# Score products of a transformer kernel: two 64-row strips per half of the heads, or four 32-row strips for both halves together

## The reference

```python
q = jnp.einsum('bsd,hdk->bhsk', query, Wq) + bq[None, :, None, :]
k = jnp.einsum('bsd,hdk->bhsk', key, Wk) + bk[None, :, None, :]
v = jnp.einsum('bsd,hdk->bhsk', value, Wv) + bv[None, :, None, :]
scores = jnp.einsum('bhqk,bhsk->bhqs', q, k) / jnp.sqrt(jnp.asarray(D_K, q.dtype))
attn = jax.nn.softmax(scores, axis=-1)
heads = jnp.einsum('bhqs,bhsk->bhqk', attn, v)
...
x = x + _L3_xattn_ref(_layernorm(x, axis=-1), ctx_1024, ctx_1024, L3_xattn_Wq, ...)
```

## Time and profile before

| | |
|---|---|
| median of 3 runs | 892.31 us (890.75 to 893.44) |
| profiled execution, its own time | 890.07 us |
| its span, first to last instruction | 888.3 us |
| PE busy | 683.0 us, 77% |
| DVE, ACT, POOL busy | 441.4, 284.9, 291.2 us |
| score products L493 | 72.5 us of records, 256 of them |
| granted TensorE clock, mean of the span | 0.837 |

### The profile page before, as it was taken

The page is one execution under the profiler, slowest core; times in us unless marked ns, Lnnn a source line. Parts: engine busy times, 40 slices in busy tenths (PEclk is TensorE's granted clock), DMA queues, the critical chain, the costliest instruction groups (busy, mean ns, idle before and its releaser), DMA issues.

```text
span 888.3 us, 15004 instructions
## 1 busy us (share of the span) xinstructions
PE 683.0 (77%) x5836; PEld 424.0 (48%) x5836; DVE 441.4 (50%) x1182; ACT 284.9 (32%) x477; POOL 291.2 (33%) x324
## 2 busy tenths in 40 slices
PE   6799733999997879997687997497657937774974
PEld 3355521774555455655344465254424533443442
DVE  5566478554444695556464465433143333233332
ACT  3133310123333424443243343133314422341432
POOL 7122211113211242322645221353254316432542
PEclk9899855899998769998598999588759866895898
DMA  6900060031000000000105300120111012101212
GB/s 141 321 2 2 25 189 8 18 130 60 1 2 1 1 0 1 1 1 22 40 23 144 85 1 2 39 39 28 39 31 36 22 33 39 31 30 30 37 33 66
DMA packets 43756, 38.98 MB, mean 44 GB/s; under 512 B 11648, under 2 KB 34720, under 8 KB 43560
## 3 DMA queue, kind: packets, MB, share of 16 engines
q1 hardware_dynamic: 37240, 26.88, 10.4%
q0 software_dynamic: 5120, 10.50, 5.3%
q10 hardware_dynamic: 1328, 0.66, 0.3%
HBM read 30.75 MB, written 7.27 MB: 43 GB/s over the span
## 4 chain that ended last, share of the span: by engine, by line
PE 66%; DVE 15%; issue 8%; DMA 4%; ACT 3%; POOL 2%; another core or an unknown queue 2%; DVEq 0%; ACTq 0%; POOLq 0%
PE psum L1586 9%; PE psum L1609 8%; PE psum L535 8%; PE psum L493 7%; PE psum L1596 5%; PE psum L557 4%; PE psum L482 3%; PE psum L782 2%; PE psum L569 2%; PE psum L1178 2%; PE psum L690 2%; PE psum L578 2%; DVE scr L906 1%; DVE scr L872 1%
## 5 line engine op out<-in xcount | busy, mean ns | idle before, releaser
L288 POOL TENSOR_TENSOR scr<-KT,hmask 128x512 f32<-128x512 f32 x64 | 67.7, 1064 | 160.3 <-PE psum L535 64.0
L405 DVE TENSOR_REDUCE Mp<-psum 128x8 f32<-128x1024 f32 x64 | 78.5, 1226 | 65.9 <-PE psum L493 28.3
L1460 DVE COPY scr<-psum 128x512 f32<-128x512 f32 x64 | 44.2, 691 | 133.7 <-PE psum L1596 102.9
L312 ACT ACTIVATE scr<-psum 128x1024 f32<-128x1024 f32 x64 | 65.5, 1023 | 121.0 <-PE psum L535 44.7
L535 PE MATMUL psum<-Qa,scr 64*128 64x128 f32 x1024 | 74.1, 285 | 0.0
L493 PE MATMUL psum<-scr 64*128 64x512 f32 x256 | 72.5, 643 | 0.0
L535 PEld LDWEIGHTS psum<-Qa,scr 64*128 64x128 f32 x1024 | 63.5, 189 | 15.6 <-issue 10.4
L1596 PEld LDWEIGHTS psum<-ident,scr 128*128 128x128 f32 x304 | 36.3, 156 | 71.3 <-issue 65.9
L1342 POOL DMA_INDIRECT yb_d<-scr,tok x44 | 42.9, 974 | 55.0 <-ACT scr L1290 49.9
L1586 PE MATMUL psum<-big,xsT 128*64 128x512 f32 x144 | 48.5, 758 | 11.8 <-issue 4.2
L1596 PE MATMUL psum<-ident,scr 128*128 128x128 f32 x304 | 56.8, 316 | 1.0 <-ACT scr L1282 0.8
(11 more groups left out here) (341 smaller groups left out, 1220.7 us busy)
## 6 DMA issues: line engine op xcount, KB each, us to landing
big<-in_L_ffn_W SPq DMA_DIRECT2D x2, 2048.0 KB, 9.0
big<-in_L_ffn_W SPq DMA_DIRECT2D x8, 512.0 KB, 9.8
big<-in_L_ffn_W SPq DMA_DIRECT2D x1, 4096.0 KB, 13.7
b1r<-in_L_ffn_b SPq DMA_DIRECT2D x1, 2048.0 KB, 10.9
scr<-yb_d SPq DMA_DIRECT2D x6, 256.0 KB, 3.1
xn_d<-xn SPq DMA_DIRECT2D x2, 512.0 KB, 3.2
scr<-ya_d SPq DMA_DIRECT2D x4, 256.0 KB, 3.0
yb_d<-scr,tok POOLq DMA_INDIRECT x44
```

What stands on the lines that cost most here:

```text
L288: pool.tensor_tensor(Km[:, i % 2, c, :, :], KT[:, c, i, :].unsqueeze(1).to_broadcast([P, HV, P]), hmask4[:, :].unsqueeze(2).to_broadcast([ ...
L312: act.activation(PT[i % 2][:, c, :], pair(weights_unit(i, c)), ACT.Exp, scale=SCALE).then_inc(S(f"exp{c}"), 1)
L405: dve.tensor_reduce(Mp[:, HC * c:HC * c + HC, DH:DH + 1], pair(scores_unit(i, c)).rearrange("p (j k) -> p j k", j=HC), AX.X, ALU.max, nega ...
L1460: ins = dve.tensor_copy(hTg[:, g % 2, :], bank[[3, 6][g % 2]])
```

## The change

The two `scores` calls of a round are replaced by two phases, `score_strips(i+1, 0)` ahead of `turn_outputs(i-2)` and `score_strips(i+1, 1)` behind it. A phase issues four products of 32 rows x 256 columns, two of each half of the heads, each on its own 32-row strip and in its own PSUM bank; the second phase takes the other strips for the same banks. DVE gets both halves of the scores when the second phase is done. The first phase waits for `Km` of both halves. The pairs of banks are handed out in the new order, and with that `weights(i, 0)` waits for `exp1` of the batch before, and the scores no longer do.

```diff
@@ -260,10 +260,10 @@
         VB = {2: 0, 3: 1}
         OB = {1: 0, 2: 1, 3: 2}
         def scores_unit(i, c):
-            return 2 * ((4 * i - 2 + 2 * c if i else c) % 3)
+            return 2 * ((4 * i - 2 + c if i else c) % 3)
         def weights_unit(i, c):
-            return 2 * ((4 * i + 3 + 2 * c) % 3)
+            return 2 * ((4 * i + 4 + c) % 3)
         def pair(u):
             return psum[:, u:u + 2, :].rearrange("p a n -> p (a n)")
@@ -482,23 +482,33 @@
                 return pe.matmul(bank[4 + n], w[:, L, HC * c:HC * c + HC, :].rearrange("p h r -> p (h r)"),
                                  src[:, 512 * h:512 * h + 512], start=True, stop=True)
-            def scores(i, c):
-                pe.wait_ge(S(f"km_ready{c}"), n0 + i + 1)
-                if i > 1:
-                    pe.wait_ge(S(f"exp{c}"), n0 + i - 1)
-                if i == 1 and c == 1:
-                    pe.wait_ge(S("max1"), n0 + 1)
-                u = scores_unit(i, c)
-                for r in range(2):
-                    ins = pe.matmul(bank[u + r], QT[64 * r:64 * r + 64, c, i, :],
-                                    Km[64 * r:64 * r + 64, i % 2, c, :, :].rearrange("p v k -> p (v k)"),
-                                    start=True, stop=L > 1, skip_group_check=L < 2)
-                if L == 1:
-                    for r in range(2):
-                        ins = pe.matmul(bank[u + r].rearrange("p (j k) -> p j k", j=4), identb[:, :],
-                                        fill[:, i, :].unsqueeze(1).to_broadcast([P, 4, P]),
-                                        start=False, stop=True, skip_group_check=True)
-                ins.then_inc(S(f"scores{c}"), 1)
+            def score_strips(i, n):
+
+                if n == 0:
+                    for c in range(2):
+                        pe.wait_ge(S(f"km_ready{c}"), n0 + i + 1)
+                    if i > 1:
+                        pe.wait_ge(S("exp0"), n0 + i - 1)
+                else:
+                    pe.wait_ge(S("scores_half"), n0 + i + 1)
+                for c in range(2):
+                    for s in (c ^ n, (c ^ n) + 2):
+                        rows = slice(32 * s, 32 * s + 32)
+                        v = 2 * (s % 2)
+                        ins = pe.matmul(bank[scores_unit(i, c) + s // 2][:, P * v:P * v + 2 * P], QT[rows, c, i, :],
+                                        Km[rows, i % 2, c, v:v + 2, :].rearrange("p v k -> p (v k)"),
+                                        start=n == 0, stop=L > 1, skip_group_check=True)
+                    if n == 1 and L != 1:
+                        ins.then_inc(S(f"scores{c}"), 1)
+                if n == 0:
+                    ins.then_inc(S("scores_half"), 1)
+                elif L == 1:
+                    for c in range(2):
+                        for r in range(2):
+                            ins = pe.matmul(bank[scores_unit(i, c) + r].rearrange("p (j k) -> p j k", j=4), identb[:, :],
+                                            fill[:, i, :].unsqueeze(1).to_broadcast([P, 4, P]),
+                                            start=False, stop=True, skip_group_check=True)
+                        ins.then_inc(S(f"scores{c}"), 1)
             def mask_zeros(i, c):
                 pe.wait_ge(S(f"zeros{c}"), i + 1)
@@ -523,11 +533,9 @@
                 if c == 0:
                     pe.wait_ge(S("qa_ready"), n0 + i + 1)
                     if i > 0:
-                        pe.wait_ge(S("max1"), n0 + i + 1)
+                        pe.wait_ge(S("exp1"), n0 + i)
                 elif i + 1 < B:
                     pe.wait_ge(S("max0"), n0 + i + 2)
-                else:
-                    pe.wait_ge(S("exp1"), n0 + i)
                 u = weights_unit(i, c)
                 for v in range(HV):
                     for r in range(2):
@@ -605,12 +613,11 @@
             queries(1)
             pe.wait_ge(S("k_copied"), 4 * L + 3)
             turn(1)
-            pe.wait_ge(S("q_copied"), 4 * L + 1)
-            scores(0, 0)
-            queries(2)
             pe.wait_ge(S("q_copied"), 4 * L + 2)
             pe.wait_ge(S("v_copied"), L + 1)
-            scores(0, 1)
+            score_strips(0, 0)
+            queries(2)
+            score_strips(0, 1)
             queries(3)
             pe.wait_ge(S("q_copied"), 4 * L + 4)
             if L == 0:
@@ -622,15 +629,15 @@
                 if here:
                     turn_maxima(i)
                 if ahead:
-                    scores(i + 1, 0)
+                    score_strips(i + 1, 0)
                 if i > 1:
                     turn_outputs(i - 2)
+                if ahead:
+                    score_strips(i + 1, 1)
                 if here:
                     weights(i, 0)
-                if ahead:
-                    if L == 0:
-                        mask_zeros(i + 1, 0)
-                    scores(i + 1, 1)
+                if ahead and L == 0:
+                    mask_zeros(i + 1, 0)
                 if 0 < i <= B:
                     attend(i - 1, 0)
                 if i > 1:
```

## The result

The changed kernel takes 913.82 us (912.99 to 917.39, 4 runs) against 892.88 us, a ratio of 1.0243 (95% interval 1.0208 to 1.0279): 20.9 us slower. The forecast was 909.7 us in a range of 903 to 922. The profiled execution went from 890.07 to 912.99 us, its span from 888.3 to 911.2. One execution of the kernel before among the experiments, of 1044.57 us at a mean granted clock of 0.61 where the others have 0.84, is left out of all ratios.

The account below looks back on a forecast made before the run. PE's queue alone was taken to set an attention round. PE savings against new waits gave 7.9 + 0.7 + 4.4 + 4.4 = 17.4 us over layers 0 to 3, on 892.31: 909.7 us, range 903 to 922.

Parts of the forecast that it names:

- What a strip phase costs: Each score phase on PE takes 0.645 us with four strips together, saving 0.63 us a round in layers 2 and 3.
- The estimate of 0.13 us more: Per strip phase, from the skill's 3.07 times speed for four row strips; 64 phases would add 8.3 us.
- The new wait for the key copy: First strip phase waits for POOL's second-half Km copy: 1.02 us a round, 1.16 in layers 1 and 0, 24 times.
- What is late next, layers 2 and 3: DVE's normalise holds out_transpose 0.50 us; rounds become 7.73 us, 4.4 us more a layer.
- Layer 1: Out_transpose not held; rounds 9.23 us, 1.65 more in five rounds, prologue and round 0 -1.0, sum 0.7 us.
- The sum: Added time over all layers: 7.9 + 0.7 + 4.4 + 4.4 = 17.4 us, feed-forward stages not touched.
- Layer 0: Second mask_zeros waits 0.85 us for DVE; rounds 10.05 us, 7.1 more in six, prologue +0.8, sum 7.9 us.
- the prologue's "+0.8": Layer 0's start: first phase needs the values too, 1.24 us later, shorter scores giving back only 0.4.
- Rival 4: Granted clock falls to 0.95 in the roughly 300 us of attention, costing some 12 us: 921; chance 0.04.
- Rival 1: The forecast itself, 909.7 us for the whole kernel, own range 904 to 917; chance 0.74.
- rivals 2 and 3: 2: strips run together only partly or in pairs, up to 936, chance 0.11; 3: key-copy wait absent or small, 884, 0.11.

Follow-up runs that it names:

- the run with all waits gone: Changed kernel plus third key buffer for the second half, DVE's normalise ahead of its score work, and both halves' zeros before the maxima in layer 0: 874.03 us, ratio 0.9806.
- the two experiments: Changed kernel with a third buffer for the second half's key copy, 884.64 us; kernel before with first-half scores also waiting for the second half's key copy, 915.05 us.
- the run with the wait alone: Kernel before with only one wait added, first-half scores waiting for the key copy of both halves: 915.05 us, ratio 1.0307.
- The run with both zeros first: Changed kernel, two key buffers, with DVE finding the zeros of both halves before the two maxima in layer 0: 907.19 us, ratio 1.0178.
- the third buffer: Changed kernel with a third buffer for the second half's key copy, so POOL need not wait for the last weights: 884.64 us, ratio 0.9954.
- normalise first: Changed kernel with DVE's normalise(i-2) ahead of its first work on batch i+1's scores in rounds 2 to 7: 905.13 us, ratio 1.0190.
- the outputs ahead: Changed kernel with turn_outputs ahead of both strip phases in PE's queue and DVE's normalise ahead of its score work: 907.50 us, ratio 1.0179.

## Why the prediction was right

**What a strip phase costs.** Right. With no wait ahead of it a phase is 0.64 us in the chain, in the run with all waits gone, where the prediction took 0.645:

```profile
364.79 0.64 PE psum L506 x8
365.44 0.59 PE psum L585 x4
366.03 0.64 PE psum L506 x8
366.67 1.09 PE psum L551 x16
```

PE's own time in a round of layer 2 fell by 6.84 - 6.22 = 0.62 us, forecast 0.63. Four strips run together at no visible loss. The estimate of 0.13 us more that the prediction worked out from the page "TensorE: Matmul & The Clock Gate" of the Trainium skill, section "Measured speedup vs the span model", is not borne out: it would make a phase 0.78 us.

**The new wait for the key copy.** Right: 0.99, 1.14 and 1.13 us a round in layers 2, 1 and 0 by the two experiments, forecast 1.02 and 1.16. It is 24 times some 1.1 us, an estimate of 26 us, by itself more than the whole result (the run with the wait alone: 27.4 us). From POOL's end to PE's load 0.07 us passed, not 0.12.

**What is late next, layers 2 and 3.** Right in place, 0.42 us instead of 0.50; the signal took 0.05 us here. Rounds 7.63 against 7.73, the layers, each with the seam ahead of it, 3.9 and 3.7 us against 4.4.

**Layer 1.** Rounds 9.25 against 9.23; the layer 0.9 against 0.7. The sum counts five rounds where the wait is in six, and its start gained 1.2 us where the sum has 1.0.

**Layer 0.** The rounds are right, 10.01 against 10.05. One was 10.39, because POOL began its copy 0.4 us late there. It did so at the same batch in the kernel before, where nothing waited for it, and in the run with the wait alone. The layer as a whole is 12.7 us in the profiled pair against 7.9. The step that went wrong is the clock, which the sum put at nothing: it takes what the change costs at the start of layer 0 from rows at the 2.4 GHz level. By `weights(0, 1)` 3.8 us were lost where the prologue's "+0.8" stands, and 1.7 more than in a normal round in round 1. From 36 to 46 us PE was granted 0.67 on the mean, that is the 1.2 GHz level for most of the time, where the kernel before was back at 2.4 GHz. Rival 4 thus came true at one place of the kernel; I had priced it for the whole attention and given it 0.04. That the time still lies in the range is owed to the range's width and to layers 2 and 3, which came out 1.3 us below their 8.8. The run with both zeros first and the table beside it tie the second fall to PE's wait for DVE.

A part of the 3.8 us seems to belong to the execution and not to the kernel. In the profiled one PE stood idle for 2.04 us ahead of its first strips, and the clock was low once more, from about 23 to 26 us. Changed kernel first, then the kernel before:

```profile
22.00:26.00 4.00, 4.00 (x19) 1.38 (x16) 0.57 (x1) 0.69 (x1) 1.34 (x2) 0.59 0.89 228
...
22.00:26.00 4.00, 3.22 (x10) 0.71 (x8) 0.96 (x1) 1.37 (x2) 1.37 (x2) 1.00 0.91 264
```

`turn_maxima(0)` came 1.96 us later than before (33.10 against 31.14). With the third buffer and with normalise first, whose PE queue is the same up to there, it came 0.35 us later and 0.14 us earlier, the idle time was 0.90 and 1.46, and the clock from 22 to 26 us was 1.00; with the outputs ahead it was as in the changed kernel. So the prologue cost no more than its "+0.8" where the clock held, and layer 0's 10 us by the medians may be the fairer number.

**The rest.** Some 1.8 us of the profiled pair lie in feed-forward stages that nobody edited; whether the difference of the medians, 20.9, has them too no run shows.

Rival 1, the forecast, came true, with rival 4 in one place; rivals 2 and 3 fell with the phase of 0.64 us and the run with the wait alone.

## What to carry to other kernels

When two pieces of work are merged, their waits are merged too, and the merged piece stands where the earlier of the two stood: list who makes each input, what that maker waits for, and how much PE work lies between. Here an input with 1.9 us to spare was needed 2.7 us earlier, and one more buffer (2 KB of a partition) turned a loss of 2.4% into a gain of 0.5%. After taking a wait away, look at the next queue: DVE's order had to follow PE's new order before the strips were worth 2%. And a sum of waits read at one granted clock misses what the waits do to the clock: look for the places where it is low before, and ask which wait beside them grows.

## What the runs showed of the hardware

- Four float32 products on four 32-row strips in four PSUM banks ran together: a phase took 0.64 us. Less the 0.20 us by which a score call behind `turn_maxima` is longer than one behind `weights` (1.06 against 0.86), that is two passes of 256 columns for all four in 0.44.
- A product that waited on the semaphore of the product just before it cost more than a change of height: two adjacent phases took 1.44 us, where 0.64 and, without a wait or a change of height, 0.43 would be 1.07. The wait is the 0.37 between, against 0.20.
- The granted clock fell to the 1.2 GHz level at 43 us in the changed kernel, behind 2.45 us in which PE stood idle, and `weights(0, 1)` took 1.93 us in place of 1.16. Behind 1.39 us of idle time at the same place in the kernel before it stayed at 2.4 GHz. The busy share from 30 to 36 us does not tell the two apart: PE was busy 4.86 of 6 us in the kernel before and 3.85 in the changed one, but 4.91 with normalise first, where the clock from 36 to 46 us was 0.76.
